# A third edge sum split in two: 1664 destinations by a weighted dense adjacency, the rest by gathering rows

## The chip, the cores and the metric

The kernel runs on one core of a Trainium2 chip. The metric is the device time in microseconds (us) of one execution; lower is better. TensorE, VectorE, ScalarE and GpSimd are called PE, DVE, ACT and POOL in the profile, and SP is the engine that does nothing but start DMAs.

## The reference

The program is two layers of a graph network over 6250 nodes of 256 features and 100,000 edges, sorted by destination, whose destinations are drawn so that low numbers are far more frequent (below node n lie about 100000 * sqrt(n / 6250) edges). Three sums over edges occur: two in the first layer, and this one in the second, with a weight for each edge:

```
feat_norm = sqrt(sum(edge_attr ** 2) + 1e-12);  w = exp(-4 * feat_norm)
agg  = segment_sum(xn[src] * w, dst);  wsum = segment_sum(w, dst)
agg  = agg / max(wsum, 1e-6)
h    = gelu(agg @ W1.T + b1);  y = xn + h @ W2.T + b2;  layernorm(y) * gamma + beta
# beside it, linear attention on the same xn:
k = elu(xn @ Wk.T) + 1;  k_sum = sum over nodes of k;  context = k.T @ v
```

## The kernel before, in words

Nodes are padded to 49 tiles of 128. Stages follow one another, each a block of instruction streams for the engines, joined by semaphores. `second_norm` adds the experts' results to the node rows, normalises them and writes two tables (`x2_tab`, `xn3_tab`); it turns the rows by PE and keeps them turned on the chip (`c.xnT`, 128x2x6272 f32). `gather_third` is the edge sum. `fold_second_attention` and `second_layer_sum` use its result.

All three edge sums go through `aggregate`. An edge tile is 128 edges, and a chunk is four tiles. For each chunk POOL gathers 4x128 rows of the node table, 1 KB each, by indirect DMA (L908) into a ring of `RING` = 5 chunks; DVE makes four one-hot matrices over a window of 128 destinations (L793 with weights in f32, L795 without in fp16); PE multiplies rows by one-hots (L755), eight f32 products a chunk in the third sum; DVE adds the window to the sums on the chip (L763). POOL may start chunk k once chunk k-5 is summed. A chunk's products wait for its rows to land, for its one-hots and for the add of the chunk before the last.

In the third sum all 196 chunks take this way. A `Side` rides in the same loop: `Keys` makes the keys of the linear attention of one node tile per four chunks: ACT copies a tile from `c.xnT` (L2676), PE multiplies (L2647), DVE and ACT make the elu (L2666, L2679, L2671), PE adds products to the attention's sums (L2655, L2658).

The first two sums gather only chunks 98 to 195. The first 1664 destinations (`ND`, 13 tiles) are summed by a dense adjacency that the class `Dense` builds in the same loop: 208 banks of eight destinations, together 710 rows of 128 edges. A row takes two one-hots from DVE (L610, L611) and one fp16 product on PE (L646) into a bank of PSUM; ACT copies the bank to an fp16 adjacency (L631); for every tile of 128 destinations 49 products 128x512 (L663) multiply it by an fp16 node table on the chip (`c.h16`, high and low halves of each feature side by side), 637 in all; DVE adds the two halves, PE turns them, DVE places them (L619, L621, L653, L600). `of_chunk` spreads the banks over the chunks by a cost per bank: early chunks get few banks of many rows, late ones three banks of two rows.

The weight sums per node come from the second gather; `second_norm` inverts them (L2533) and spreads them over the partitions into `c.agg[:, 2]` (L2497), and `second_layer_sum` multiplies on POOL (L2832).

## Time and profile before

| | us |
|---|---|
| Median of 3 runs (lowest, highest) | 4871.57 (4865.47, 4884.47) |
| Profiled execution, its own time | 4901.53 |
| Its span, first to last instruction | 4899.9 |
| Mean granted PE clock, share of full | 0.81 |
| First gather stage, about | 411 to 1124 |
| Second gather stage, about | 1478 to 2093 |
| `second_norm` | 2916 to 3102 |
| Third gather | 3106.2 to 4251.7 |

A time in the trace is counted from the span's start. "Busy" is the time in which at least one instruction of a group runs; "mean" is the length of one, and pipelined instructions overlap, so that count times mean can exceed busy. The idle time of a group is what its engine spent just before its instructions, by what ended it; "issue" is time in which the engine waited for nothing the profile shows, "remote" a release that the profile doesn't name. SPq is SP's queue.

### The profile page before, as it was taken

To read this page: it belongs to the slowest core of one execution; us is meant where nothing else is said; L and a number is where in the kernel's file an instruction comes from. 1 tells how busy PE (TensorE), PEld (TensorE's weight loads), DVE (VectorE), ACT (ScalarE), POOL (GpSimd) and SP (SyncE) were. 2 spreads that over 40 slices of the span, in tenths; PEclk is the share of its full clock that TensorE was granted. 3 is DMA by queue.
4 is the path that set the end of the run, shared out by engine and by line. 5 is a ranking of instruction groups with operands and counts; after the bars stand their busy time and mean duration, and the time that the engine had idled before them with its cause. 6 is when DMAs were issued, how large, how long until landed. Compare 5 with 4: busy or idle time off the path is not lost. (4 is left out here: it accounts for less than half of the span.)

```text
span 4899.9 us, 68142 instructions
## 1 busy us (share of the span) xinstructions
PE 3243.4 (66%) x21190; PEld 2392.1 (49%) x21191; DVE 2407.5 (49%) x7608; ACT 968.5 (20%) x1999; POOL 1955.0 (40%) x2055
## 2 busy tenths in 40 slices
PE   2534888886995768754068861365555656599798
PEld 2422454543564445544057751355555555466554
DVE  7947777663226666566134444322222222277654
ACT  1102222320120112222123322000000000033454
POOL 1013555550005666511711126566666666533100
PEclk8656899997996989976579985677777777789899
DMA  4104232221013323244421117433333333301100
GB/s 122 65 33 144 81 87 84 83 82 48 12 36 99 87 87 87 84 155 160 147 68 64 64 51 227 124 96 97 97 95 97 97 96 95 95 30 45 31 23 26
DMA packets 239100, 416.62 MB, mean 85 GB/s; under 512 B 39042, under 2 KB 171590, under 8 KB 237607
## 3 DMA queue, kind: packets, MB, share of 16 engines
q0 software_dynamic: 90720, 247.45, 17.2%
q1 hardware_dynamic: 141100, 158.88, 9.9%
q10 hardware_dynamic: 7068, 7.60, 0.5%
q8 instruction: 116, 1.90, 0.2%
q14 instruction: 96, 0.79, 0.1%
HBM read 328.87 MB, written 84.91 MB: 84 GB/s over the span
## 5 line engine op out<-in xcount | busy, mean ns | idle before, releaser
L755 PE MATMUL psum<-scr 128*128 128x128 f32 (+1 forms) x5880 | 749.7, 293 | 346.4 <-issue 198.3
L908 POOL DMA_INDIRECT scr<-xn_table,src_i x784 | 746.5, 952 | 410.4 <-issue 239.9
L755 PEld LDWEIGHTS psum<-scr 128*128 128x128 f32 (+2 forms) x5880 | 700.1, 184 | 404.3 <-issue 380.5
L908 POOL DMA_INDIRECT scr<-h_table,src_i x392 | 376.5, 960 | 515.8 <-issue 387.4
L908 POOL DMA_INDIRECT xnT<-xn_table,src_i x392 | 374.1, 954 | 422.2 <-PE psum L755 226.2
L763 DVE TENSOR_TENSOR agg<-agg,psum 128x256 f32 x196 | 82.1, 419 | 728.0 <-remote 538.4
L646 PE MATMUL psum<-scr 128*128 128x98 f16 (+3 forms) x1420 | 262.2, 255 | 262.3 <-DVE scr L611 150.2
L610 DVE TENSOR_SCALAR scr<-iota,scr 128x128 f16<-128x128 bf16 x1420 | 375.0, 272 | 94.7 <-remote 42.7
L611 DVE TENSOR_SCALAR scr<-expert_scores,scr 128x98 f16<-128x98 f16 (+3 forms) x1420 | 397.8, 291 | 1.9 <-issue 1.9
L646 PEld LDWEIGHTS psum<-scr 128*128 128x128 f16 x1420 | 128.5, 100 | 432.0 <-DVE scr L611 229.2
L793 DVE TENSOR_SCALAR scr<-iota,dloc,w_edge 128x128 f32<-128x128 f32 x784 | 221.0, 367 | 83.3 <-issue 77.3
L2435 PE MATMUL psum<-scr,xnT 128*128 128x128 f16 x2544 | 200.4, 234 | 63.1 <-issue 58.6
L2679 ACT ACTIVATE scr<-scr 128x256 f32<-128x256 f32 x49 | 20.4, 416 | 1104.7 <-DVE scr L2666 625.8
L3502 PE MATMUL psum<-scr 128*128 128x512 f16 (+2 forms) x1197 | 209.0, 329 | 16.6 <-ACT scr L3440 9.8
L2435 PEld LDWEIGHTS psum<-scr,xnT 128*128 x2544 | 178.3, 104 | 82.1 <-issue 68.1
L2344 POOL DMA_DIRECT2D expert_results<-scr x106 | 57.3, 541 | 398.6 <-DVE scr L2395 398.6
L1410 PE MATMUL psum<-xnT,scr 128*128 128x512 f32 x392 | 197.7, 650 | 22.0 <-issue 17.7
L631 ACT ACTIVATE agg<-psum 128x392 f16<-128x392 f32 x208 | 103.3, 497 | 524.3 <-PE psum L646 427.9
L631 ACT ACTIVATE scr<-psum 128x392 f16<-128x392 f32 x208 | 100.6, 496 | 497.8 <-PE psum L646 274.1
L663 PE MATMUL psum<-xnT,scr 128*128 128x512 f16 x637 | 181.6, 408 | 3.5 <-DVE agg L600 3.5
L663 PE MATMUL psum<-scr,agg 128*128 128x512 f16 x637 | 173.0, 392 | 0.6 <-DVE agg L600 0.6
L2421 PE MATMUL psum<-ident,scr 128*128 128x128 f32 x212 | 42.3, 284 | 195.2 <-DMA scr<-expert_rows 195.2
(442 smaller groups left out, 5814.6 us busy)
## 6 DMA issues: line engine op xcount, KB each, us to landing
scr<-expert_rows SPq DMA_DIRECT2D x106, 128.0 KB, 2.0
expert_results<-scr POOLq DMA_DIRECT2D x106, 128.0 KB, 2.1
scr<-xn_table,src_i POOLq DMA_INDIRECT x784
agg<-in_L_ffn_W SPq DMA_DIRECT2D x16, 512.0 KB, 9.8
x_table<-scr SPq DMA_DIRECT2D x14, 512.0 KB, 3.0
xn_table<-scr SPq DMA_DIRECT2D x14, 512.0 KB, 4.5
scr<-xn_table SPq DMA_DIRECT2D x14, 512.0 KB, 3.9
scr<-x_table SPq DMA_DIRECT2D x14, 512.0 KB, 4.9
```

Of the source, the lines that this page charges most:

```text
L610: v.tensor_scalar(self.place_hot[:, u, :], c.iota16[:], self.lists[:, 1, r:r + 1], None, ALU.is_equal)
L611: v.tensor_scalar(self.code_hot[:, u, 0:wide], c.iota_wide[:, 0:wide], self.lists[:, 0, r:r + 1], None, ALU.is_equal).then_inc(self.rows_h ...
L631: a.activation(self.adjacency[:, tile % 2, :, q * BN:(q + 1) * BN], self.c.psum[:, 5 + t % 2, 0:BN * HI].rearrange("p (n h) -> p h n", h=H ...
L646: pe.matmul(c.psum[:, 5 + t % 2, at:at + wide * HI], self.place_hot[:, n % self.ring, :], self.code_hot[:, n % self.ring, 0:wide * HI], st ...
L663: last = pe.matmul(c.psum[:, 7, :], self.adjacency[:, tile % 2, h, :], self.x16[:, h, :], start=(h == 0), stop=(h == HI - 1))
L755: last = pe.matmul(bank[b][:, s, :], lhs, hot[:, hot_b, t, :], start=(t == 0 and n == 0), stop=(t == CT - 1 and n == pieces - 1))
L763: return v.tensor_tensor(window, window, bank[b], ALU.add)
L793: last = v.tensor_scalar(hot[:, b, t, :], iota[:], dst(t), weight(t), ALU.is_equal, ALU.mult)
L908: g.indirect_dma_start(out=rows[:, u, t, :], out_offset=None, in_=table, in_offset=bass.IndirectOffsetOnAxis(ap=index(t), axis=0)).then_in ...
L1410: ins = pe.matmul(c.psum[:, 2 + half, :], tile[:, k, :], wkv[:, k, half * 512:(half + 1) * 512], start=(k == 0), stop=(k == 1))
L2435: last = pe.matmul(c.psum[:, 2 + b, m * P:(m + 1) * P], c.w1_16[:, ds(e, 1), k, wp, m * P:(m + 1) * P].rearrange("p e n -> p (e n)"), xT[: ...
L3502: last = pe.matmul(out, weights(wp), moving(xp), start=(first and i == 0), stop=(k_last and i == 2))
```

## The change

`gather_third` gets the form of the first two: chunks 98 to 195 are gathered, and the 1664 first destinations are summed by `WeightedDense`. Since the sum must hold f32 accuracy with weights, each row's place one-hot carries the edge's weight, scaled and already divided by the destination's weight sum, as an fp16 number, and ACT makes a second one with the fp16 rest; PE multiplies both. A bank then holds f32 values: ACT copies them to fp16 (high), and DVE subtracts that from the bank into a second fp16 adjacency (low). For each of 637 slices PE multiplies the high part by 512 columns and the low part by 256. The placed window is written, not added. `second_norm` prepares this: it loads the edge lists, divides the weights, splits them, writes the fp16 node table over `c.xnT`, and sends the turned rows to a table in DRAM (`xnT_tab`), from which `Keys` now loads its tiles (L2676 goes); `Keys` takes two chunks a tile in place of four. `fold_second_attention` loads the weight sums' inverse and the turned rows back. The ring of gathered rows has four chunks.

What moves on PE, in the middle of the third gather. Before, eight L755 are a chunk, L2647 the keys' product, L2655 and L2658 their sums:

```order
L2655 MATMUL psum<-scr 128x256 x2
L2658 MATMUL psum<-ones,scr 128x1 x2
L755 MATMUL psum<-scr 128x128 x8
L2647 MATMUL psum<-scr 128x256 x2
L755 MATMUL psum<-scr 128x128 x24
L2655 MATMUL psum<-scr 128x256 x2
```

Now, late in the stage, where L870 is the chunk, L759 and L762 are a row's two products (high and low weight), L773 and L775 a slice by the high and by the low adjacency:

```order
L759 MATMUL psum<-scr 128x392
L762 MATMUL psum<-scr 128x392
L773 MATMUL psum<-xnT,agg 128x512
L775 MATMUL psum<-xnT,scr 128x256
L773 MATMUL psum<-xnT,agg 128x512
L775 MATMUL psum<-xnT,scr 128x256
L773 MATMUL psum<-xnT,agg 128x512
L775 MATMUL psum<-xnT,scr 128x256
L870 MATMUL psum<-scr 128x128 x8
L2862 MATMUL psum<-scr 128x256 x2
L2865 MATMUL psum<-ones,scr 128x1 x2
L759 MATMUL psum<-scr 128x392
```

Between two chunks PE now has one to five such turns, and a step of the keys after every chunk.

On SP's queue, from the third gather's end to the constants of the last stage, before:

```order
L2708 DMA scr<-turned_weights 128x512 x2
L2703 UNCONDITIONAL_BRANCH
L2803 UNCONDITIONAL_BRANCH
L2806 DMA scr<-turned_weights 128x512 x3
L2809 DMA scr<-in_L_gnn_b 128x256
```

and now:

```order
L2923 DMA scr<-turned_weights 128x512 x2
L2925 DMA agg<-wsum_row 128x896
L2927 DMA xnT<-xnT_table 128x2x896
L2925 DMA agg<-wsum_row 128x5376
L2927 DMA xnT<-xnT_table 128x2x5376
L2918 UNCONDITIONAL_BRANCH
```

Four loads, 9.6 MB together, stand on the queue ahead of the last stage's constants.

The diff, cut to its core:

```diff
+HOTR3, RING3 = 8, 4
+WSCALE = 2.0 ** 15
...
+            gathered = c.base[:, FIRST // CT:NC]
+            step.done(v.tensor_scalar(gathered, gathered, float(ND), None, ALU.max))
...
+class WeightedDense(Dense):
...
+    def vector(self, v, t):
+        c = self.c
+        tile = self.places(t)
+        if tile is not None:
+            v.wait_ge(self.turned, tile + 1)
+            v.tensor_scalar(c.agg[:, 0:2, tile * P:(tile + 1) * P], c.psum[:, 7, 0:2 * P].rearrange("p (k n) -> p k n", n=P),
+                            1.0 / (XS * WSCALE), None, ALU.mult).then_inc(self.placed, 1)
+        if 0 <= t - 2 < NB:
+            v.wait_ge(self.taken, t - 1)
+            v.tensor_tensor(self.nodes(self.low, t - 2), self.bank(t - 2), self.nodes(self.adjacency, t - 2), ALU.subtract
+                            ).then_inc(self.lowered, 1)
+        if t < NB:
+            for r in BANK_ROWS[t]:
+                n = self.row_at[r]
+                u = n % self.ring
+                if n >= self.ring:
+                    v.wait_ge(self.rows_used, n - self.ring + 1)
+                wide = HI * ROW_OF[r][1]
+                v.tensor_scalar(self.place_hot[:, u, 0, :], c.iota16[:], self.list_at("low", r), self.list_at("weight", r),
+                                ALU.is_equal, ALU.mult)
+                v.tensor_scalar(self.code_hot[:, u, 0:wide], c.iota_wide[:, 0:wide], self.list_at("code", r), None,
+                                ALU.is_equal).then_inc(self.rows_hot, 1)
+        self.add_halves(v, t)
...
+    def scalar(self, a, t):
+        if 0 <= t - 1 < NB:
+            tile, q = divmod(t - 1, BPT)
+            a.wait_ge(self.rows_used, self.row_at[BANK_ROWS[t - 1][-1]] + 1)
+            if tile >= 2 and q == 0:
+                a.wait_ge(self.sliced, (tile - 1) * self.SLICES)
+            a.activation(self.nodes(self.adjacency, t - 1), self.bank(t - 1), ACT.Copy).then_inc(self.taken, 1)
+        if t < NB:
+            for r in BANK_ROWS[t]:
+                n = self.row_at[r]
+                u = n % self.ring
+                a.wait_ge(self.rows_hot, n + 1)
+                a.activation(self.place_hot[:, u, 1, :], self.place_hot[:, u, 0, :], ACT.Copy, scale=self.list_at("ratio", r)
+                             ).then_inc(self.rows_low, 1)
+    def tensor(self, pe, t):
+        c = self.c
+        if t < NB:
+            for r in BANK_ROWS[t]:
+                n = self.row_at[r]
+                node, wide, k, count = ROW_OF[r]
+                at = (node % BN) * HI
+                u = n % self.ring
+                pe.wait_ge(self.rows_hot, n + 1)
+                if r == BANK_ROWS[t][0] and t >= 2:
+                    pe.wait_ge(self.lowered, t - 1)
+                out = c.psum[:, 5 + t % 2, at:at + wide * HI]
+                pe.matmul(out, self.place_hot[:, u, 0, :], self.code_hot[:, u, 0:wide * HI], start=(k == 0), stop=False,
+                          skip_group_check=True)
+                pe.wait_ge(self.rows_low, n + 1)
+                pe.matmul(out, self.place_hot[:, u, 1, :], self.code_hot[:, u, 0:wide * HI], start=False,
+                          stop=(k == count - 1), skip_group_check=True).then_inc(self.rows_used, 1)
+        self.turn_sums(pe, t)
...
             for h in range(HI * q // self.SLICES, HI * (q + 1) // self.SLICES):
-                last = pe.matmul(c.psum[:, 7, :], self.adjacency[:, tile % 2, h, :], self.x16[:, h, :], start=(h == 0),
-                                 stop=(h == HI - 1))
+                pe.matmul(c.psum[:, 7, :], self.adjacency[:, tile % 2, h, :], self.x16[:, h, :], start=(h == 0), stop=False,
+                          skip_group_check=True)
+                last = pe.matmul(c.psum[:, 7, 0:D], self.low[:, tile % 2, h, :], self.x16[:, h, 0:D], start=False,
+                                 stop=(h == HI - 1), skip_group_check=True)
...
-                    if dense and dense.placed_by[min(k + 2, n_chunks)]:
-                        v.wait_ge(dense.placed, dense.placed_by[min(k + 2, n_chunks)])
...
-                        g.wait_ge(summed, fast.summed(k - RING + 1))
+                    if k >= ring:
+                        g.wait_ge(summed, fast.summed(k - ring + 1))
...
-            sp.dma_start(c.agg[:, 2, :], c.wsum_row.partition_broadcast(P)).then_inc(w_out, 16)
+            sp.dma_start(inverse, c.wsum_dense.partition_broadcast(P)).then_inc(inverse_in, 16)
+            sp.wait_ge(w_vec, 4)
+            sp.dma_start(wsum_rows[0:DT, :], dense_scale[0:DT, :]).then_inc(w_out, 16)
+            sp.dma_start(wsum_rows[DT:NT, :], wsum[DT:NT, :]).then_inc(w_out, 16)
...
-            v.memset(c.agg[:, 0:2, :], 0.0)
...
+            v.memset(c.agg[:, 0:2, ND:NP], 0.0)
+            step = Chain(v, listed)
+            v.wait_ge(lists_in, 16)
+            step.done(v.tensor_tensor(by_place, c.iota[:, 0:BN].unsqueeze(1).broadcast_to([P, ROWS, BN]),
+                                      place.unsqueeze(2).broadcast_to([P, ROWS, BN]), ALU.is_equal))
+            step.wait()
...
+                last = v.tensor_tensor(of_bank, of_bank, nodes.unsqueeze(2).broadcast_to([P, e - b, m, BN]), ALU.mult)
...
+            step.done(v.tensor_reduce(of_row, by_place, AX.X, ALU.add))
+            step.wait()
+            step.done(v.scalar_tensor_tensor(w_valid, w_valid, WSCALE, of_row, ALU.mult, ALU.mult))
+            step.wait()
+            step.done(v.tensor_copy(high16, w_valid))
+            step.wait()
+            step.done(v.tensor_copy(high, high16))
+            step.wait()
+            step.done(v.tensor_tensor(rest, w_valid, high, ALU.subtract))
+            step.done(v.tensor_scalar(of_row, high, 1e-30, None, ALU.max))
+            step.wait()
+            step.done(v.reciprocal(of_row, of_row))
+            step.wait()
+            for slot, j, values in ((0, 0, code), (0, 1, low), (1, 0, high)):
+                v.tensor_copy(c.list_parts[slot][:, :, j], values)
+            v.tensor_tensor(c.list_parts[1][:, :, 1], rest, of_row, ALU.mult)
...
+            def low_part(s, h):
+                nt = HALVES[h][1]
+                v.wait_ge(high_ready, s * 2 + h + 1)
+                tiles16 = rows16[:, ds(s * TS + HALVES[h][0], nt), :]
+                v.scalar_tensor_tensor(tiles16[:, :, D:2 * D], xn3[:, h, 0:nt, :], XS, tiles16[:, :, 0:D],
+                                       ALU.mult, ALU.subtract).then_inc(low_ready, 1)
...
+                if former is not None:
+                    low_part(*former)
...
+            def spill(s, h):
+                t0, nt = HALVES[h]
+                a.wait_ge(copied, s * 2 + h + 1)
+                a.dma_start(turned_tab[:, :, ds(s * SS + t0 * P, nt * P)], xn3T[:, h, :, 0:nt * P]).then_inc(spilled[h], 16)
+            def unit(s, h, former, last):
+                t0, nt = HALVES[h]
+                if not last:
+                    a.wait_ge(vec, s * (2 * PER) + h * PER + 2)
+                    indices(s + 1, h)
+                if former is not None:
+                    spill(*former)
+                a.wait_ge(vec, s * (2 * PER) + h * PER + 5)
+                a.activation(rstd[:, h, 0:nt], rstd[:, h, 0:nt], ACT.Sqrt).then_inc(root, 1)
+                a.wait_ge(vec, s * (2 * PER) + (h + 1) * PER)
+                a.activation(rows16[:, ds(s * TS + t0, nt), 0:D], xn3[:, h, 0:nt, :], ACT.Copy, scale=XS).then_inc(high_ready, 1)
+                a.wait_ge(turned, s * 2 + h + 1)
+                a.wait_ge(spilled[h], s * 16)
+                for k in range(2):
+                    ins = a.activation(xn3T[:, h, k, 0:nt * P], c.psum[:, 2 * h + k, 0:nt * P], ACT.Copy)
+                ins.then_inc(copied, 1)
...
+    hot, rows_f = part.take([HOTS, CT, W]), part.take([RING3, CT, D])
+    wk, tile, rows = c.m0, part.take([2, P]), part.take([D])
     low, e, kk = part.take([D]), part.take([D]), part.take([D])
-    beyond = part.take([ET - FIRST])
+    place_hot, code_hot = part.take([HOTR3, 2, P], F16), part.take([HOTR3, BN * HI], F16)
+    adjacency_low = part.take([2, HI, P], F16)
+    adjacency = c.agg[:, 2, :].bitcast(F16).rearrange("p (a h n) -> p a h n", a=2, h=HI)
...
-            v.tensor_scalar(beyond, c.dloc[:, FIRST:ET], 0.0, MASKED, ALU.is_lt, ALU.mult).then_inc(unmasked, 1)
-            v.wait_ge(unmasked, 1)
-            v.tensor_tensor(c.dloc[:, FIRST:ET], c.dloc[:, FIRST:ET], beyond, ALU.add)
...
-        turn, steps = 4, 0
+        turn, steps = 2, 2
...
-            if u == 0:
-                a.wait_ge(z_ready, i)
-                a.activation(tile[:], c.xnT[:, :, ds(i * P, P)], ACT.Copy).then_inc(tile_ready, 1)
-            if u == 1:
+            if u == 1 and new:
...
+            sp.dma_start(tile, turned_tab[:, :, 0:P]).then_inc(tile_ready, 16)
+            sp.dma_start(rows, c.xn3_tab[0:P, :]).then_inc(rows_ready, 16)
+            with sp.Fori(1, NT) as i:
+                sp.wait_ge(z_ready, i)
+                sp.dma_start(tile, turned_tab[:, :, ds(i * P, P)]).then_inc(tile_ready, 16)
                 sp.wait_ge(sums_done, i)
                 sp.dma_start(rows, c.xn3_tab[ds(i * P, P), :]).then_inc(rows_ready, 16)
-    aggregate(c, c.xn3_tab, hot, rows_f, split=False, weighted=True, slots=(0, 1), side=Keys())
+    dense = WeightedDense(c, "conv3", c.h16, adjacency, adjacency_low, c.list_parts, place_hot, code_hot,
+                          NC - FIRST // CT, HOTR3)
+    aggregate(c, c.xn3_tab, hot, rows_f, split=False, weighted=True, slots=(0, 1), side=Keys(), dense=dense,
+              start=FIRST // CT, unset=c.agg[:, 0:2, 0:ND])
...
+            for n, nodes in enumerate((slice(0, SS), slice(SS, NP))):
+                sp.dma_start(c.agg[:, 2, nodes], c.wsum_row[:, nodes].partition_broadcast(P)
+                             ).then_inc(c.last_wsum_loaded[n], 16)
+                sp.dma_start(c.xnT[:, :, nodes], c.xnT_tab.rearrange("p (k n) -> p k n", k=2)[:, :, nodes]
+                             ).then_inc(c.last_xnT_loaded[n], 16)
...
+                g.wait_ge(c.last_wsum_loaded[0 if isinstance(s, int) and s == 0 else 1], 16)
...
+                pe.wait_ge(c.last_xnT_loaded[0 if isinstance(s, int) and s == 0 else 1], 16)
```

## Rows read from the trace of the kernel before

**Rows 1.** Stretches: length, busy PE, PEld, DVE, ACT, POOL, PE clock, DMA share, GB/s.

```profile
411.00:1124.00 713.00, 589.62 (x3668) 343.58 (x3667) 479.45 (x2180) 176.24 (x352) 374.07 (x392) 0.91 0.29 83
...
1478.00:2093.00 615.00, 446.61 (x4117) 309.49 (x4117) 380.38 (x1949) 100.60 (x208) 376.47 (x392) 0.87 0.30 86
...
2915.90:3102.20 186.30, 24.54 (x98) 18.97 (x98) 85.63 (x206) 34.09 (x68) 110.27 (x99) 0.50 0.60 191
...
3106.20:4251.70 1145.50, 682.40 (x3728) 619.58 (x3726) 315.47 (x1078) 36.53 (x99) 746.49 (x784) 0.75 0.33 96
```

**Rows 2.** Groups by line, third gather; busy us, mean ns, idle before.

```profile
L908 POOL DMA_INDIRECT scr<-xn_table,src_i x784 | 746.5, 952 | 410.4 <-issue 239.9 <-remote 139.7 <-PE psum L755 30.9
...
L793 DVE TENSOR_SCALAR scr<-iota,dloc,w_edge 128x128 f32<-128x128 f32 x784 | 221.0, 367 | 83.3 <-issue 77.3 <-PE psum L755 3.0 <-PEq L2616 3.0
```

**Rows 3.** Timeline of the third gather near its end: start, length, engine, line.

```profile
4242.84 1.03 PE L2647 MATMUL psum<-scr 128*128 128x256 f32 x4
...
4246.61 0.42 DVE L2666 TENSOR_SCALAR scr<-psum 128x256 f32<-128x256 f32 x1
...
4246.84 3.81 PE L755 MATMUL psum<-scr 128*128 128x128 f32 x32 [1.20 <-DVE agg L763]
...
4250.49 1.03 PE L2655 MATMUL psum<-scr 106*128 106x256 f32 x4
...
4251.35 0.50 PE L2658 MATMUL psum<-ones,scr 106*128 106x1 f32 x4
```

**Rows 4.** Timeline of the second gather, which has the dense part.

```profile
1800.90 0.34 PE L646 MATMUL psum<-scr 128*128 128x98 f16 x4
...
1801.08 1.03 PE L663 MATMUL psum<-xnT,scr 128*128 128x512 f16 x4
...
1807.20 1.87 PE L663 MATMUL psum<-xnT,scr 128*128 128x512 f16 x4
...
1704.62 0.24 DVE L610 TENSOR_SCALAR scr<-iota,scr 128x128 f16<-128x128 bf16 x1
...
1704.78 0.24 DVE L611 TENSOR_SCALAR scr<-expert_scores,scr 128x98 f16<-128x98 f16 x1
```

**Rows 5.** Groups of the second gather by line and form.

```profile
L631 ACT ACTIVATE scr<-psum 128x392 f16<-128x392 f32 x208 | 100.6, 496 | 497.8 <-PE psum L646 274.1 <-remote 183.1 <-issue 35.9
...
L762 DVE SCALAR_TENSOR_TENSOR agg<-psum,agg 128x384 f32 x98 | 54.0, 551 | 70.9 <-remote 46.4 <-PE psum L755 24.0 <-DVE agg L600 0.5
```

**Rows 6.** Waits in the first gather: who waited for whom, us, times, longest.

```profile
DVE xnT L1426 <- ACT xnT L1447: 126.1, 37, 5.4
```

**Rows 7.** Timeline in the experts' stage: four ScalarE operations.

```profile
2906.20 1.14 ACT L2361 ACTIVATE scr<-psum,feature_columns 128x128 f32<-128x128 f32 x4 [3.70 <-PE psum L2435]
```

**Rows 8.** Timeline of the start of the normalisation.

```profile
2929.50 11.68 POOL L2523 DMA_INDIRECT scr<-expert_results,scr  x1 [0.30 <-issue]
...
2929.75 10.51 DVE L2529 MEMSET agg<- 128x12544 f32 x1 [14.60 <-issue]
...
2943.02 0.35 SPq L2497 DMA_DIRECT2D agg<-wsum_row  x1
...
2959.49 1.23 DVE L2539 TENSOR_TENSOR scr<-scr 128x1024 f32<-128x1024 f32 x1 [18.17 <-DMA scr<-x_table]
```

**Rows 9.** Lengths: DVE over all 5680 list elements; a reciprocal.

```profile
L1214 DVE TENSOR_TENSOR agg<-agg x1: 6077/6077/6077, 331.7 to 331.7; 128x5680 f32<-128x5680 f32 x1
...
L2908 DVE RECIPROCAL scr<-scr x14: 303/328/353, 4284.6 to 4567.3; 128x32 f32<-128x32 f32 x7, 128x24 f32<-128x24 f32 x7
```

**Rows 10.** Timeline: a 3136 KB load and its wait; the last stage's constants.

```profile
2092.62 0.32 SPq L1773 DMA_DIRECT2D scr<-dis_row  x1
...
2104.75 13.29 DVE L1781 TENSOR_TENSOR agg<-agg,scr 128x6272 f32<-128x6272 f32 x2 [12.41 <-DMA wsum_row<-agg]
...
4252.13 0.81 SPq L2708 DMA_DIRECT2D scr<-turned_weights  x2
...
4270.11 6.15 PE L3087 MATMUL psum<-xnT,scr 128*128 128x512 f32 x8 [9.91 <-DMA scr<-in_L_ffn_gW]
```

288 lines of the change are left out of this document (175 added, 113 removed).

## The prediction, made before the changed kernel ran

> **What bounds the kernel now.** I read the busy times by stretch first, then, for the third gather, its groups by line and its timeline, and beside it the same views of the first two gathers, which already have a dense part. The table of stretches [rows 1] shows the third gather as much the longest stage, 1145.5 us, with PE 60% busy at a mean granted clock of 0.75, DVE 28% and POOL 65%. POOL's group [rows 2] says what the stage runs on: 784 gathers of 0.952 us with about 0.3 us between two, so 1.25 us each at best, and waits on top for chunks summed ("remote" and PE L755). 1145.5 / 784 = 1.46 us for a gather; the DMA moves 96 GB/s meanwhile. So the stage is bound by gathers and their landing, and PE and DVE wait for them. The second gather [rows 1] has 392 gathers with the dense part beside them in 615 us, 1.57 us each, hardly more; the first one has 392 in 713 us, 1.82 each, and there PE (590 busy) and DVE (479) are fuller. The change turns the third stage into the form of these two, with more arithmetic than either.
>
> **The change part by part.** The profiled execution took 4901.53 us against a median of 4871.57 for the runs shown. The sum is made on the profiled execution, and the difference is taken from the median.
>
> *Gathers.* 392 instead of 784. By the present rate 392 x 1.46 = 572 us, by POOL's own pace 392 x 1.25 = 490. These are floors of the new stage; the question is whether PE or DVE is now above them. The ring of four chunks instead of five leaves POOL three chunks ahead; at over 7 us a chunk (below) that is over 21 us for four gathers of 5 us in all, so I price it at nothing; if PE were fast again, its cost would be the gathers' rate.
>
> *PE at full clock.* A chunk's eight f32 products: two chunks in 3.81 us [rows 3], 1.9 each, x 98 = 187 us. Slices: four of 512 columns take 1.03 us at the full clock and 1.87 at half [rows 4], so what scales with the clock is 0.84 / 4 = 0.21 us each; 637 x 0.21 = 134, and 637 of 256 columns half of it, 67. Row products: four of 98 columns begin within 0.18 us (1800.90 to 1801.08, [rows 4]), 0.045 each. The 710 rows are 16 of 49 columns, 323 of 98, 285 of 196 and 86 of 392, each now twice, together 244,000 columns: 112 us. Keys: 1.03 + 1.03 + 0.50 [rows 3] x 49 = 125. Turning the tiles, about 6. Sum 631 us. That is above both floors: PE becomes the bound.
>
> *DVE.* Row one-hots start 0.16 us apart [rows 4]. The place one-hot now has two scalar operands and a multiplication, a form the trace has only in f32, 0.367 us [rows 2]. Its bounds are 0.16 and 0.37; I take 0.2. 710 x (0.2 + 0.16) = 256. The 208 subtractions from a PSUM bank of 392 columns: nearest is L762, 0.55 us at 384 columns [rows 5], 114. Chunk one-hots 392 x 0.28 (221.0 / 784 [rows 2]) = 110. Window adds, keys' two steps, tile sums and placing: 98 + 98 + 39 of 0.42 [rows 3] = 99. Sum 579, bounds 551 to 700. So DVE lies beside PE, 50 us below it, but not evenly: `of_chunk` gives the first 18 chunks 6 to 34 rows with few slices, where DVE is longer, and the late ones three turns, where PE is (8 us against 5.5). Taking the larger of the two chunk by chunk costs about 25 us over PE's sum.
>
> *ACT.* Low one-hots 710 x 0.285 (1.14 / 4 [rows 7]) = 202, banks 208 x 0.496 [rows 5] = 103, exponentials 49 x 0.42 = 20: 325, far from a bound. But it stands in the chain: it copies bank t-1 only after PE has finished it, and makes the low one-hots of turn t after that, some 0.5 + 0.1 + 0.3 us, and 0.285 a row. PE has 3.5 slices x 0.315 = 1.1 us to cover the first; a second or third turn in one chunk with four rows loses some 0.4 us. I take 33 us for all. The very first bank has 34 rows, each going DVE, ACT, PE before the first chunk can be summed: 34 x 0.45 = 15 us at the start.
>
> *Clock.* It was 0.91 and 0.87 in the first two gathers and 0.75 in this one [rows 1]. PE will be fuller than in the first, so 0.93: 631 / 0.93 = 678. The stage: 678 + 25 + 33 + 15 = 751, with a few us to drain 755 us. Saved: 1145.5 - 755 = 390. Bounds of the stage: 680 (PE alone) to 878 (rival one).
>
> *The normalisation.* At the start DVE clears two thirds of `agg` in 10.5 us, and POOL's gather beside it takes 11.68 instead of 0.95 [rows 8]. The new clearing is 9216 of 12544 columns, 7.7 us. Behind it, in one chain on DVE before the first unit: three passes over 5680 elements at 6.1 [rows 9], the middle one in eight pieces (+1), 19; a reciprocal of 710 elements at (353 - 303) / 8 = 6.2 ns each [rows 9], 4.5; ten operations on 710 elements at 0.5 to 0.9, 7; small ones and waits, 2. From 2929.75 that ends at 2970; the first unit began at 2959.49, when its rows landed [rows 8]: +10. Their load will land earlier, as the 3.2 MB spread no longer stands ahead of it, so nothing else is late. In the seven passes each adds 2 DVE operations for the low rows of the table (1.23 at 1024 columns [rows 8], 0.9 at 768) and 0.9 MB of turned rows sent out on ACT's queue into a stage that moves 191 GB/s: 4.8 us of traffic, of which I take 2 as not hidden. 7 x 4 = 28, and 2 for the last spill. The fp16 copies on ACT lie in its wait for PE's turning. Sum +40; bounds +12 (start alone) to +75 (all of the traffic too, and ACT in the chain).
>
> *The fold.* SP works its loads in order: the first rows of the normalisation, asked for just behind the 3.2 MB spread of 2943.02, landed after 16 us [rows 8]. A 3136 KB load took 12.1 us from issue to its waiter [rows 10], about 3.8 us a MB. The change puts 9.6 MB on the queue at 4253; at 3.1 to 3.8 us a MB they are in at 4283 to 4289, and the last stage's constants come behind, 4 us. PE now begins that stage at 4270.11 [rows 10], waiting for just these constants. +21; bounds 0 (the later loads overtake) to +30.
>
> *The rest.* Two DVE operations at the start of the third gather go, -1. The ACT copy of the keys' tile and the gathers' window waits lay beside other work: 0. In the first two gathers waits between DVE's own operations go: 0 to -3.
>
> Sum: -390 + 40 + 21 - 1 = -330. 4871.57 - 330 = **4541 us**.
>
> A rule of the Trainium skill speaks against this change. First the row: POOL's gathers take 0.954 and 0.960 us in the first two stages, beside 1420 and more one-hots of 16-bit numbers each, and 0.952 in the third, with none of that form (busy over count [rows 1]). So small one-hots don't hold POOL here, though the long clearing did [rows 8]. SBUF — State Buffer, "Who interferes with whom", says that VectorE in a two-port perf mode and GpSimd lock each other out of a shared port pair for a whole instruction; taken for every one-hot it would give rival three.
>
> **The rivals.**
>
> *One: the engines don't overlap as well as summed.* The first gather by the same prices: an f32 product costs about four times an fp16 one of as many columns, so the four key and value products of 512 columns are 4 x 4 x 0.21 = 3.4 us a tile, 167 for 49; four f32 products of 128 for each tile, some 1.1 us, 54; slices 134; rows 56; 98 chunks of 16 fp16 products of 128, 16 x 0.053, 83; 6 for turning: 500 us of PE. The stage took 713, 1.4 times as much. At that ratio 631 gives 883, 128 us more: 4669. Against it: there DVE sat idle 126 us for ACT's squares of the same step [rows 6], which held up its dense turns; the new keys leave a chunk between PE's product, DVE and ACT. For it: the new turn waits on DVE, ACT and PE in a ring, and the first stage's clock of 0.91 is in that ratio too.
>
> *Two: gathers still bound.* If row and slice products hide in the weight loads' shadow, the stage falls to 392 x 1.46 = 572 to 1.57 x 392 = 615 as in the second gather: saving 530 to 573, 4871.57 - 550 + 60 = 4382. Against: PE's sum is a count of columns.
>
> *Three: DVE and POOL exclude one another.* 392 x 0.95 = 372 us of POOL beside 579 of DVE, one after the other: 951, 4737. Against: the stages above.
>
> *Four, slower than before: PE stays at the lower clock level, 1.2 GHz, through the stage.* In the third gather now the mean is 0.75, so it is at each of its two levels half of the time; a chunk in the middle of the stage is as often slow as fast. With small waits inside every turn it may not come up. 631 x 2 + 73 = 1335 us, 190 more than now, plus 60: 5121. It decides from a mean clock of 631 / (1145 - 60 - 73) = 0.62 downwards. Against: in both stages with the dense part the clock is higher, not lower [rows 1].
>
> *Five: the change doesn't take effect*, as when the flag sends the sums down their slow way; then the time would be many times this. The dense part covers all edges of its destinations by the counts, and chunk 98 begins near node 1574, below 1664: 0.01.
>
> **How the numbers follow.** Forecast 0.68 (its own range 4470 to 4625), rival one 0.16, two 0.07, three 0.04, four 0.03, five 0.01, and 0.01 for a gain in the stage eaten by an unseen cost elsewhere to within nothing. The range that leaves out two in ten reaches over rival one's size but not over two or three: 4440 to 4685. Half a percent, 24 us, is about what a measurement tells from no change here. Faster by more: 0.95; within: 0.01; slower: 0.04.
>
> **What would show it.** The new third gather at 755 us with PE busy over 85% and a clock over 0.9; POOL waiting for PE in nearly every chunk, not for landings. Late chunks longer (about 8.5 us) than middle ones (about 7); were they alike at 6, gathers bind. DVE's idle before its bank subtractions and the row products' idle "<-ACT" give the ring's price (33 us). The one-hot with two scalars: near 0.2 us apart. The first unit of the normalisation 10 us later, a pass of it 4 us longer. PE's first product of the last stage some 20 us behind the fold's end. Wrong would be a stage under 680 (PE's prices too high) or a clock under 0.8.

## The result and the profile after

The changed kernel takes 4527.3 us, the median of four runs (4524.13 to 4538.25), against 4868.52 for the kernel before on the same chip (four runs, 4863.0 to 4884.47): a ratio of 0.9297, 95% interval 0.9274 to 0.9321, so 341 us less. 4541 was predicted, 330 less. The profiled execution took 4538.25 us, with a span of 4536.6.

The stretches of the changed kernel, in the columns of [rows 1]: length, busy time of PE, PEld, DVE, ACT and POOL, granted clock, DMA share, GB/s.

```profile
411.00:1475.00 1064.00, 881.98 (x4688) 528.63 (x4687) 587.24 (x2361) 230.69 (x426) 380.48 (x395) 0.91 0.23 68
1475.00:2091.10 616.10, 444.90 (x4117) 305.87 (x4117) 380.43 (x1949) 100.45 (x208) 375.55 (x391) 0.87 0.31 90
2903.30:3109.80 206.50, 24.54 (x98) 18.98 (x98) 127.16 (x242) 33.28 (x71) 114.10 (x100) 0.51 0.62 199
3114.20:3869.50 755.30, 681.97 (x4877) 510.80 (x4876) 574.40 (x2255) 353.20 (x968) 374.05 (x392) 0.93 0.30 86
3870.00:3904.00 34.00, 4.46 (x15) 3.21 (x14) 2.38 (x8) 0.00 (x0) 2.37 (x2) 0.50 0.93 361
3904.00:4536.00 632.00, 562.37 (x2716) 357.47 (x2716) 381.91 (x712) 275.50 (x435) 110.62 (x70) 0.90 0.10 32
```

The third gather is the fourth line: 755.3 us where it was 1145.5 [rows 1], PE busy 90% at a clock of 0.93, DVE 76%, POOL down from 746 to 374. The fold, the fifth line, is new as a stretch with DMA busy 0.93 of the time.

The waits of that stage, by who waited for whom (us, times, longest):

```profile
POOL scr L1020 <- PE psum L870: 256.9, 85, 11.6
DVE scr L714 <- ACT agg L737: 66.9, 50, 3.1
PEld psum L762 <- ACT scr L743: 52.3, 157, 6.8
PE psum L762 <- ACT scr L743: 19.7, 30, 6.7
PE psum L759 <- DVE scr L726: 17.8, 12, 2.8
```

POOL waits 85 times, in 98 chunks, for PE to have summed a chunk. PE is now what the others wait for. The groups of the stage that carry the prediction's prices (busy, mean ns of one, idle before):

```profile
L743 ACT ACTIVATE scr<-scr,agg 128x128 f16<-128x128 f16 x710 | 247.3, 394 | 63.7 <-DVE scr L726 41.3 <-issue 17.4
L724 DVE TENSOR_SCALAR scr<-iota,agg 128x128 f16<-128x128 bf16 x710 | 228.5, 325 | 33.8 <-remote 17.2 <-issue 9.2 <-PE psum L762 7.4
L762 PE MATMUL psum<-scr 128*128 128x98 f16 (+3 forms) x710 | 156.6, 247 | 31.1 <-ACT scr L743 19.7 <-issue 3.3
L714 DVE TENSOR_TENSOR scr<-psum,agg 128x392 f16<-128x392 f32 x208 | 116.9, 562 | 67.8 <-ACT agg L737 66.9 <-issue 0.7
```

**Where the time went.** Between fixed marks of the two profiled executions: up to the experts' last send (POOL, 2915.90, now 2903.30) -12.6; from there to the third gather's first one-hot 190.3, now 210.9 (+20.6); the third gather to the fold's first copy 1146.0, now 756.4 (-389.6); the fold to PE's first product of the last stage 17.9, now 33.3 (+15.4); the rest +2.9. Together -363.3. The two medians are 341 apart: the profiled execution of before was 30 us above its median, that of after 11. So about 20 us of the sum of the marks belongs to the two executions, and the first term, -12.6, is not larger than that.

### The profile page after: what moved, and what is told of

Read it like the earlier page. It is cut to its first block and busy times, and to the rows that moved or that the text cites. A ratio compares the mean times of both kernels' runs of the same rounds, so it can differ in the third digit from the quotient of the medians.

```text
span 4536.6 us, 72069 instructions
## 1 busy us (share of the span) xinstructions
PE 3246.4 (72%) x22342; PEld 2281.7 (50%) x22343; DVE 2707.3 (60%) x8818; ACT 1283.5 (28%) x2871; POOL 1587.1 (35%) x1664
## 3 DMA queue, kind: packets, MB, share of 16 engines
q0 software_dynamic: 71904, 196.05, 14.6%
## 5 line engine op out<-in xcount | busy, mean ns | idle before, releaser
L1020 POOL DMA_INDIRECT scr<-xn_table,src_i x392 | 374.0, 954 | 382.3 <-PE psum L870 256.9
L870 PE MATMUL psum<-scr 128*128 128x128 f16 (+1 forms) x4312 | 409.3, 258 | 7.4 <-remote 5.0
L870 PEld LDWEIGHTS psum<-scr 128*128 128x128 f16 (+2 forms) x4312 | 390.4, 145 | 39.0 <-issue 11.4
L743 ACT ACTIVATE scr<-scr,agg 128x128 f16<-128x128 f16 x710 | 247.3, 394 | 63.7 <-DVE scr L726 41.3
L724 DVE TENSOR_SCALAR scr<-iota,agg 128x128 f16<-128x128 bf16 x710 | 228.5, 325 | 33.8 <-remote 17.2
L773 PE MATMUL psum<-xnT,agg 128*128 128x512 f16 x637 | 222.3, 387 | 0.6 <-DVE agg L710 0.6
L726 DVE TENSOR_SCALAR scr<-expert_scores,agg 128x98 f16<-128x98 f16 (+3 forms) x710 | 197.6, 280 | 0.0
L2507 DVE SCALAR_TENSOR_TENSOR scr<-psum,scr 128x256 f32<-128x256 f32 x106 | 45.0, 425 | 240.1 <-PE psum L2560 240.1
```

Source lines behind the costliest of these rows:

```text
L724: v.tensor_scalar(self.place_hot[:, u, 0, :], c.iota16[:], self.list_at("low", r), self.list_at("weight", r), ALU.is_equal, ALU.mult)
L743: a.activation(self.place_hot[:, u, 1, :], self.place_hot[:, u, 0, :], ACT.Copy, scale=self.list_at("ratio", r)).then_inc(self.rows_low, 1)
L773: pe.matmul(c.psum[:, 7, :], self.adjacency[:, tile % 2, h, :], self.x16[:, h, :], start=(h == 0), stop=False, skip_group_check=True)
L870: last = pe.matmul(bank[b][:, s, :], lhs, hot[:, hot_b, t, :], start=(t == 0 and n == 0), stop=(t == CT - 1 and n == pieces - 1))
L1020: g.indirect_dma_start(out=rows[:, u, t, :], out_offset=None, in_=table, in_offset=bass.IndirectOffsetOnAxis(ap=index(t), axis=0)).then_in ...
```

## The experiments

They ran on three chips, which are of two kinds by the kernel before. "The second chip" stands for two of them: experiments 1 to 4 ran on one, where the kernel before takes 4617 us, and 9 to 12 on the other, where it takes 4612. Experiments 5 to 8 ran on a chip where it takes 4872; which chip gave the result above is not recorded, but the 4869 us there are alike, and both are called "the first chip". Each ratio is to the kernel before on the same chip, and stage lengths are compared within one of the two kinds.

**1. No low one-hots** (second chip). In the third gather ACT makes no low one-hot and PE reads the high one again (the low half of the weights is left out; the scale is halved).

```
-                pe.wait_ge(self.rows_low, n + 1)
-                pe.matmul(out, self.place_hot[:, u, 1, :], ...
+                pe.matmul(out, self.place_hot[:, u, 0, :], ...
-                a.activation(self.place_hot[:, u, 1, :], self.place_hot[:, u, 0, :], ...
```

> ACT makes no low one-hots; the second row product of TensorE reads the high one-hot again, so PE has all its products and the ring DVE - ACT - PE of a row is cut by ACT (the low half of the weights is left out). Changed kernel: 4527 us, third gather 755 us. Theory A (prediction: the ring costs 33 us beside PE's sum): 4494, stage about 722. Theory B (PE is nearly the whole bound, 682 of 755 us busy, and its idle time is the start and the end of the stage): at most 12 us less, 4515 to 4527. Theory C (ACT's copies of banks come late because they stand behind the one-hots): over 45 us less.

4336.8 us, ratio 0.9395 (0.9379 to 0.9410); the stage took 685.3 us against 714.3 in experiment 3, which has this stage as the changed kernel. 29 us: theory A. The edit takes away ACT's work and PE's wait for it together; experiments 7, 9 and 10 ask which of them counts.

**2. No low slices** (second chip). The 256-column products of the adjacency's low half are left out, and that part of the sum with them.

```
-                pe.matmul(c.psum[:, 7, :], self.adjacency[...], self.x16[:, h, :], start=(h == 0), stop=False, ...
-                last = pe.matmul(c.psum[:, 7, 0:D], self.low[...], self.x16[:, h, 0:D], start=False, ...
+                last = pe.matmul(c.psum[:, 7, :], self.adjacency[...], self.x16[:, h, :], start=(h == 0), stop=(h == HI - 1), ...
```

> The 637 products of 256 columns with the low half of the adjacency are left out (so is that part of the sum). Theory A (prediction: PE is the bound, each costs its columns, 0.105 us at full clock): 67 / 0.95 = 70 us less, 4457, and the stage near 685 with PE still over 85% busy. Theory B (these products hide behind the weight loads of 0.10 us): their whole price is the load, same order, 60 to 70 us, but not told apart by this. Theory C (the ring of DVE, ACT and PE binds, PE's share is only full by chance): under 30 us less, and PE's busy share falls to under 85%.

4319.8 us, ratio 0.9358 (0.9343 to 0.9374); the stage took 674.0, 40 less, between A and C. The stretches tell why (experiment 2, then 3; columns as above):

```profile
3150.00:3300.00 150.00, 141.29 (x1056) 103.67 (x1055) 140.12 (x583) 91.46 (x251) 88.24 (x94) 0.95 0.36 102
3450.00:3600.00 150.00, 138.78 (x902) 94.79 (x902) 120.92 (x445) 74.72 (x196) 77.47 (x82) 0.97 0.31 91
```

```profile
3150.00:3300.00 150.00, 143.38 (x1155) 109.70 (x1153) 135.34 (x563) 88.25 (x245) 86.13 (x92) 0.97 0.35 100
3450.00:3600.00 150.00, 141.30 (x998) 106.59 (x997) 110.53 (x409) 69.19 (x182) 71.47 (x75) 0.95 0.29 82
```

In the first half DVE is busy 135 of 150 us beside PE, and with the slices gone 140. Counted by the chunks' window additions, 34 of 42 us come from the last 52 chunks and 7 from the first 45: in the chunks before them DVE is about as near to being the bound as PE.

**3. The large loads later** (second chip). Nothing is left out.

```
             for n, nodes in ((0, slice(0, SS)), (1, slice(SS, NP))):   # fold_second_attention: now n = 0 only
...
             for h in range(2):
                 load(0, h, True)
+            load_last(c, sp, 1, slice(SS, NP))    # second_layer_sum: wsum_row and xnT_table
```

> The two large loads of the fold (8.2 of 9.6 MB, nodes after the first 1024 or so) are issued on the same queue behind the last stage's constants and first rows; nothing is left out. Changed kernel: PE's first product of the last stage comes 33.4 us after the fold's first DVE copy, before 18. Theory A (the constants stand in one queue behind the 9.6 MB): 12 to 17 us less, 4510 to 4515, that stretch back at 18 to 21 us. Theory B (the time goes to the DMA engines' total traffic in this place, whatever the order): no change, since the same bytes are moved in the same time, 4525. Theory C (the second pass of the last stage then waits for its rows behind 8 MB): what is gained at the start is lost by 3990.

4349.8 us, ratio 0.9424 (0.9409 to 0.9440). SP's issues in the changed kernel, and PE's first product of the last stage (start, length):

```profile
3870.62 0.69 DVE L2932 COPY scr<-psum 128x512 f32<-128x512 f32 x1 [4.69 <-PEq L898]
3873.17 0.58 SPq L2927 DMA_DIRECT2D xnT<-xnT_table  x1
3882.46 4.21 SPq L3029 DMA_DIRECT2D scr<-in_L_mix_bproj  x1
3886.71 6.32 SPq L3029 DMA_DIRECT2D scr<-in_L_ffn_gb  x1
3893.07 3.21 SPq L3030 DMA_DIRECT2D scr<-in_L_ffn_gW  x1
3903.95 6.46 PE L3309 MATMUL psum<-xnT,scr 128*128 128x512 f32 x8 [25.21 <-DMA scr<-in_L_ffn_gW]
```

And with the loads later:

```profile
3715.40 0.43 SPq L3031 DMA_DIRECT2D scr<-in_L_mix_bproj  x1
3715.88 0.43 SPq L3031 DMA_DIRECT2D scr<-in_L_ffn_gb  x1
3716.35 0.43 SPq L3032 DMA_DIRECT2D scr<-in_L_ffn_gW  x1
3722.36 2.93 PE L3312 MATMUL psum<-xnT,scr 128*128 128x512 f32 x3 [10.68 <-DMA scr<-in_L_ffn_gW]
```

Behind the large loads even the issuing of a small one takes 3 to 6 us instead of 0.43. The fold, from its first copy (3703.64 here) to that product, falls to 18.7 us, from 33.3 in the changed kernel and 33.2 in experiment 4 on this chip: theory A. It stays gained: experiment 4, which lacks this edit, is 17.4 us longer.

**4. Gathers held back at the start** (second chip).

```
                 for k in range(n_chunks):
+                    if k == 1 and dense and not dense.loads:
+                        g.wait_ge(dense.rows_used, len(BANK_ROWS[0]))
```

> In the third gather POOL issues the first chunk's four gathers and then waits until the 34 rows of the first bank have been multiplied, before it goes on; nothing is left out. In the changed kernel the first 22 rows take 7 us, then seven come 1.0 to 3.0 us apart with DVE idle and nobody late, until POOL has filled its ring (last gather at 3133.05), and the first chunk is summed 27 us after the stage begins, where 15 were predicted. Theory A (DVE's instructions come in by DMA and are held up by the gathers' transfers): the 34 rows take about 14 us, the stage begins 8 to 13 us earlier, 4515 to 4519. Theory B (the instructions are late whatever POOL does): no gain, or 5 us lost since chunks 1 to 3 land later, 4527 to 4532.

4367.3 us, ratio 0.9458 (0.9443 to 0.9474). The edit could not be judged: on this chip the first bank's rows took 12.9 us with it and 13.0 without it (experiment 3). On the first chip they took 26.4 to 26.9 in all five profiles of kernels with this stage. DVE's one-hots there, in the changed kernel:

```profile
3122.75 0.32 DVE L724 TENSOR_SCALAR scr<-iota,agg 128x128 f16<-128x128 bf16 x1 [0.96 <-PE psum L762]
3127.68 0.31 DVE L724 TENSOR_SCALAR scr<-iota,agg 128x128 f16<-128x128 bf16 x1 [2.33 <-remote]
3131.18 0.33 DVE L724 TENSOR_SCALAR scr<-iota,agg 128x128 f16<-128x128 bf16 x1 [3.02 <-remote]
3137.20 0.31 DVE L724 TENSOR_SCALAR scr<-iota,agg 128x128 f16<-128x128 bf16 x1
3140.60 3.16 DVE L908 TENSOR_SCALAR scr<-iota,dloc,w_edge 128x128 f32<-128x128 f32 x12
```

From 3121 to 3137 a row comes every 0.6 to 3.5 us, with PE and ACT waiting for DVE; from 3137 on it is 0.38 again, 4 us after POOL's last gather (3133.05) into the filled ring. That DVE's instructions reach it late beside the gathers would fit, but was not shown.

**5. The changed kernel again** (first chip).

> The changed kernel once more, as the reference of the runs beside it, on the chip where they run. On the chip of the last four runs the kernel before took 4617 us where it took 4869 before, and the second gather 496 us where it took 587 to 596. Theory A (there a gather lands as fast as POOL issues it, 1.27 us, so that the kernel before gains most in its third gather of 784): changed kernel 4362 to 4370 and a ratio of 0.945, the gain 250 us instead of 341. Theory B (all stages are faster alike): ratio 0.93.

4531.2 us, ratio 0.9295 (0.9279 to 0.9311), third gather 751.1 us. It is the reference for 6 to 8, and the expectation's figure for the second chip was not tested by it; there experiment 4, whose edit moved nothing, stands nearest, at 0.9458.

**6. The waits put back** (first chip) into the first two gathers.

```
             v.wait_ge(self.turned, tile + 1)
+            v.wait_ge(added, settled)
...
+                    if dense and dense.loads and dense.placed_by[min(k + 2, n_chunks)]:
+                        v.wait_ge(dense.placed, dense.placed_by[min(k + 2, n_chunks)])
                     add_window(v, ...)
```

> The changed kernel with the waits put back that the first two gathers had between DVE's own operations (on the last window added, and on the tile placed); nothing is left out. In the first pair of profiles the changed kernel reached the end of the experts 12.6 us earlier, 4 us of it in the first gather and 8 to 9 in the second; predicted were 0 to 3. Theory A (these waits are the cause): 8 to 13 us more than the changed kernel, a ratio to before higher by 0.002 to 0.003. Theory B (the difference is that of two executions or of code positions, and the waits cost 0 to 3 us): same time within 3 us.

4527.5 us, ratio 0.9297 (0.9280 to 0.9313), not told from experiment 5: theory B. The clearing begins at 2918.5, as in the changed kernel (2920.2 and 2919.0).

**7. Low products two rows behind** (first chip), with the edit of experiment 3. A region of the bank is now begun before the one ahead of it has had its low product, and the sums come out changed; the work is the same, and the time is what is read.

```
+                behind.append(r)
+                if len(behind) > 2:
+                    low_product(behind.pop(0))
+            for r in behind:
+                low_product(r)
```

> Two edits: the fold's two large loads behind the last stage's constants (alone: PE's first product 18.7 us after the fold's start, not 33.4), and PE multiplies a row's low one-hot two rows later than its high one, so that it does not wait for ACT inside a bank; nothing is left out. Without ACT's one-hots the third gather took 685 us against 714. Theory A (the 29 us are PE waiting for ACT row by row): the stage falls by 15 to 25 us to 690 to 700 on that chip, the whole 28 to 40 below the changed kernel. Theory B (the 29 us come at the end of a bank: last low product, ACT's copy, DVE's subtraction, then the slices): 5 us or less from this edit, and 13 to 20 for both.

4509.3 us, ratio 0.9255 (0.9242 to 0.9267), 22 below experiment 5. By the marks, the fold gave 14.8 of it (33.6 to 18.8) and the last stage 7.4; the third gather took 752.8 against 751.1. So nothing from this edit: theory B. PEld's wait for ACT ahead of the low product fell from 46.9 to 21.1 us, and its wait for DVE ahead of the high product rose from 17.6 to 37.5: the wait only moved.

**8. Twice the turned rows** (first chip) sent out in the normalisation.

```
                 a.dma_start(turned_tab[...], xn3T[:, h, :, 0:nt * P]).then_inc(spilled[h], 16)
+                a.dma_start(again_tab[...], xn3T[:, h, :, 0:nt * P]).then_inc(spilled[h], 16)
```

> In the normalisation each turned tile is sent out twice, the second time to a table of its own, on the same queue (0.9 MB more a pass, 6.4 MB in all). Predicted was 4 us a pass for the added work, 2 of them for this traffic; measured were about 1.4 a pass in all, counted from the experts' end to the third gather 20 us, 10 of them at the start. Theory A (the traffic costs its bytes at the stage's 191 GB/s, 4.8 us a pass, of which half shows): 14 us more, 28 with ACT's queue waiting for it. Theory B (loads and sends have room, the pass is set by its chain): 0 to 4 us more.

4534.0 us, ratio 0.9307 (0.9291 to 0.9322), not told from experiment 5. By the marks, the first unit to the third gather's first one-hot takes 167.9 us against 156.5: 11.4, or 1.6 a pass. In the whole they don't show: in this profiled execution the third gather is 2 us shorter and the last stage 6. Between A and B.

**9 and 10. One wait a row; one wait for two rows** (second chip, both with the edit of experiment 3). PE waits for ACT's low one-hot alone, ahead of both products, for one row or for two.

```
-                pe.wait_ge(self.rows_hot, n + 1)
+                if (r - BANK_ROWS[t][0]) % 2 == 0:      # 1 in experiment 9
+                    pe.wait_ge(self.rows_low, min(n + 2, self.row_at[BANK_ROWS[t][-1]] + 1))
...
-                pe.wait_ge(self.rows_low, n + 1)
```

> The fold's loads reordered as before (14.6 us by its stretch), and PE waits once a row in place of twice: only for ACT's low one-hot, which is itself made after the high one, ahead of both products (710 waits fewer); nothing is left out. On the chip of the reference run the changed kernel takes 4531 us and its third gather 751 to 756 (749 to 753 in its variants); without ACT's one-hots, and with one wait a row, the stage was 29 us shorter, 0.4 us a chunk also in the late chunks of six rows. Theory A (the second wait between two short products costs PE about 0.04 us, since it breaks the run of weight loads and products): the stage falls by 20 to 30 us, the whole 35 to 45 below the changed kernel. Theory B (ACT's own time counts: the bank's copy stands behind its one-hots, and frees the bank late): stage unchanged or up to 20 us longer, as the high product now waits for ACT too; the whole 0 to 15 below.

> As the one with one wait a row, but PE waits for two rows at once (355 waits), then issues four products; nothing is left out. Theory A (each wait costs PE about 0.04 us): 10 to 14 us less than with one wait a row, 45 to 60 below the changed kernel. Theory B (the chain through DVE and ACT counts, and PE now starts a bank one row later, about 0.4 us for each of 208 banks where it is not hidden): the same as with one wait a row or up to 40 us more.

One wait a row: 4350.0 us, 0.9426 (0.9413 to 0.9439), the same as experiment 3. 710 waits fewer gave none of the 20 to 30 us of theory A, which falls. That a wait costs nothing is not quite shown, since the high product now waits for ACT too: PE's idle time ahead of the row products is 37.7 us, against 32.3 in experiment 3. For pairs: 4374.3 us, 0.9483 (0.9470 to 0.9496), 24 more. The same idle time is 69.4 us: ahead of a bank's first product 45.4 in place of 27.2, and ahead of its later pairs 24.0 in place of 10.5. So the later one-hots cost, and the larger part of it at a bank's start. The stage in experiments 9 and 10:

```profile
2991.30:3705.20 713.90, 666.71 (x4880) 497.16 (x4878) 571.52 (x2255) 361.25 (x968) 373.11 (x392) 0.96 0.32 91
```

```profile
2989.90:3729.00 739.10, 662.11 (x4880) 504.28 (x4878) 573.30 (x2255) 358.56 (x968) 373.29 (x392) 0.94 0.31 88
```

Equal work, 25 us apart. Counted by the chunks' window additions, 17.7 of 24.6 fall into the last 52, where 20 of experiment 1's 29 fell too.

**11. Clearing later** (second chip), with the edits of experiment 10.

```
-            v.memset(c.agg[:, 0:2, ND:NP], 0.0)
             step = Chain(v, listed)
...
             unit(0, 1, (0, 0))
+            v.memset(c.agg[:, 0:2, ND:NP], 0.0)
```

> As with pairs, and the clearing of agg (7.74 us) is moved from ahead of the lists to behind the second unit of the normalisation; nothing is left out. Theory A (the start's one chain on DVE sets the first unit, and a pass of 21 us has room for 7.7 us of DVE, which is 127 of 206 us busy): 7 to 8 us less. Theory B (it moves into a pass that DVE's chain sets, and a gather of POOL beside it takes 12 us instead of 1): 0 to 2 us less or some us more.

4367.4 us, 0.9466 (0.9453 to 0.9479), 6.9 less than experiment 10, whose highest and lowest runs (4369.7 to 4380.6) overlap these (4363.1 to 4370.4) by 0.7. From DVE's first instruction to the first unit it is 33.5 us against 40.3, and to the third gather 6.3 less: theory A, though by the runs alone the two would hardly be told apart.

**12. The kernel before again** (second chip), one run.

> The kernel before once more, for its profile. The changed kernel twice reached its 7.7 us clearing at 2919 to 2920, the kernel before its 10.5 us clearing at 2929.75, and the waits put back did not bring these 10 us back. Theory A (they are the difference of one execution): the clearing of this run begins between 2917 and 2923. Theory B (they belong to the kernel before, by the windows of the first two gathers that it adds below node 1664, or by where its code lies): again 2927 to 2932, the second gather 596 us against 587.

4612.8 us. The clearing begins at 2797.9, and in the changed kernel's variants of that chip at 2800 to 2805 behind 3 us of new small work: no 10 us here, so theory A as far as this chip goes; the kernel before was not profiled again on the first chip, where the 10 us were. Its third gather, and POOL's waits in it; then those on the first chip, with PE's wait for DVE, which has no counterpart on the second:

```profile
2971.30:3964.60 993.30, 655.58 (x3728) 601.88 (x3726) 318.81 (x1077) 36.15 (x98) 746.21 (x784) 0.80 0.38 111
```

```profile
POOL scr L908 <- issue: 248.6, 758, 18.0
POOL scr L908 <- PE psum L755: 7.9, 26, 0.3
```

```profile
POOL scr L908 <- issue: 239.9, 720, 19.2
POOL scr L908 <- remote: 139.7, 51, 4.4
POOL scr L908 <- PE psum L755: 30.9, 13, 3.4
PE psum L755 <- DVE agg L763: 134.4, 35, 15.4
```

On the second chip POOL hardly waits for PE: 784 gathers in 993 us, 1.27 each, its own pace. There the changed stage (714 us) saves 279, not 390, and the whole some 250.

What held the stage on the first chip was not the landing of the rows. The last DMA packet of a gather ends 1.48 us (median) after POOL's instruction on the first chip and 1.47 on the second. But PE's first product of a chunk follows the chunk's landing by 11.3 us (median) on the first and by 0.43 on the second. POOL waits for a summed chunk, and there PE is late. One chunk's products on the first chip, whose rows had landed at 3691.4, and one on the second, whose rows landed at 3485.2:

```profile
3704.95 0.19 PEld L755 LDWEIGHTS psum<-scr 128*128 128x128 f32 x1 [0.94 <-issue]
3705.66 0.27 PE L755 MATMUL psum<-scr 128*128 128x128 f32 x1 [1.16 <-issue]
3706.37 0.36 PE L755 MATMUL psum<-scr 128*128 128x128 f32 x1 [0.44 <-issue]
3709.18 0.37 PE L755 MATMUL psum<-scr 128*128 128x128 f32 x1 [1.83 <-issue]
```

```profile
3485.79 3.65 PE L755 MATMUL psum<-scr 128*128 128x128 f32 x16 [2.36 <-issue]
```

Inside a chunk nothing makes PE wait, and yet it stops. Counted over the stage, PE is idle 133 times for over 0.3 us, 125.8 us in all, ahead of products that wait for nothing; in the third gather of experiment 12 and in that of the changed kernel, on either chip, never. The stage is 152 us longer than on the second chip. Why PE stops on the first chip, and why in the changed kernel it doesn't, stays open.

## Why the prediction was right, step by step

**Gathers as a floor.** Right for the new stage: 392 x 1.25 = 490 is below it, and POOL waits for PE. The reading of the old stage was wrong: 1.46 us a gather was put down to gathers and their landing, with PE and DVE waiting for them. On this chip POOL waited for PE, which stopped without a cause that the profile shows (12). The pace of POOL alone gives 993 us, as on the second chip. The forecast took the 1145.5 us as measured, so the wrong reading did it no harm here.

**PE's sum.** 631 us at full clock and 0.93 gave 678; PE is busy 682 at 0.93. Leaving out the low slices gives back 40 us and not their 70, since DVE is close behind.

**DVE's sum.** 579; measured 574. The one-hot with two scalars stands 0.22 ahead of its fellow, 0.2 taken; the subtraction takes 0.562, 0.55 taken. ACT's low one-hots run 0.29 apart; ACT is busy 353, of 325.

**Unevenness, ring, start.** +25 + 33 + 15 were added to 678. The ring's price is 29 us (experiment 1). Its place was given as single rows and turns; fewer waits of PE (9) and another order inside a bank (7) gave nothing, and later one-hots cost 24 us (10), more at a bank's start than behind it. Which link of DVE, ACT and PE is last was not separated. The start was mis-sized: 26.4 us where 15 was taken; on the second chip 13.0. That the stage came out at 756.4 of 755 is luck in part. Beside PE's busy time 73 us are left, just the 73 that were added. But on the second chip, in experiment 4, the stage takes 711.8 with PE busy 668.0, and 44 are left: 29 for the ring and 13 for the start leave 2 for the unevenness, an estimate, where 25 were taken. The first chip's stage is 44 us longer than that: 13 at the start, 29 in the next 45 chunks and 2 in the rest, and no term stood for that. By the window additions, chunks 60 to 90 take 8.0 us, 30 to 60 take 7.2, and the first thirty 7.3 on the first chip and 6.5 to 6.6 on the second; predicted were 8.5 for late and 7 for middle ones.

**Clock.** Right at 0.93; rival four, at half clock, was far off.

**Normalisation.** +40 predicted, +20.6 by the marks, the step's size being wrong. The start was right: the first unit comes 53.5 us behind the experts' last send, before 43.6, so +9.9 for 10. Two small errors cancel in it: the clearing begins 3 us later by small work ahead of it that had no term, and from there to the first unit it takes 36.6 us where 40 were added up. Its chain on DVE in the changed kernel:

```profile
2920.16 7.74 DVE L2675 MEMSET agg<- 128x9216 f32 x1 [1.87 <-issue]
2927.82 6.00 DVE L2679 TENSOR_TENSOR scr<-iota,agg 128x5680 f32<-128x5680 f32 x1
2933.86 6.56 DVE L2691 TENSOR_TENSOR scr<-scr,agg 128x272 f32<-128x272 f32 x8
2940.45 6.07 DVE L2695 TENSOR_REDUCE agg<-scr 128x710 f32<-128x5680 f32 x1
2950.01 4.59 DVE L2706 RECIPROCAL agg<-agg 128x710 f32<-128x710 f32 x1
2956.76 1.22 DVE L2724 TENSOR_TENSOR scr<-scr 128x1024 f32<-128x1024 f32 x1
```

The passes were not: 157.4 us from the first unit to the third gather against 146.7, 1.5 us a pass in place of 4. Doubling the traffic costs 1.6 a pass (8), so the 2 us for the traffic look about right, and the DVE operations priced beside it, 2 a pass, hidden; no run left those out.

**Fold.** +21 predicted, +15.4 measured, 14.6 given back by the order of the loads (3). The mechanism stood as written; 3.1 to 3.8 us a MB was too dear, since at the 361 GB/s that the stretch moved a MB takes 2.8. PE's product comes 24.5 us behind the fold's last copy, where 20 were named as the sign.

**The first two gathers.** 0 to -3; the marks show -12.6, but the waits put back cost nothing (6), and it does not come back on the second chip (12). Where the 12.6 come from on the first is open.

**The rivals.** One would need 1.4 times PE's sum; it is 1.20. Two fell: the slice products have their price (2), and POOL waits for PE. Three fell too: POOL's gathers take 0.954 us beside 2255 DVE instructions (374.0 / 392).

**The sum.** Against the marks' -363 the predicted -330 is short by 33: 19 in the normalisation, 6 in the fold, 11 ahead of the experts' end, less 3 in the last stage. Against the medians' -341 it is short by 11, since 22 belong to the two profiled executions. The third gather's -390 has no part in it.

**A version faster than both.** Experiment 3 alone: 0.9424 on the second chip, where the changed kernel's nearest stand-in has 0.9458. Its loads with the later clearing of 11 would be some 7 us better by the two runs; the pair was not run.

## What to carry to other kernels

Price the engine that will bind after the change by counting its columns and rows, and check the bound you remove as well: a rate of 1.46 us a gather looked like landings, and the time from landing to first use (11.3 us, against 0.43 on another chip) says that it was not. What there was to save differed by 110 us between two chips. Large loads for later belong behind the small ones needed next, in the same queue. In a ring over three engines take away work and add latency in separate runs: the busy shares do not show which of the two is paid for.

## What the hardware showed that was not expected

The prediction took it from [rows 8] that the clearing holds up POOL. In the changed kernel a gather that starts 1.8 us into it takes 12.69 us, though the one before it, also inside it, takes 0.95; and it ends 0.8 us behind the list comparison that follows. With the clearing moved (experiment 11), the same 7.74 us have five gathers of 0.94 to 0.95 inside them, and a long gather of 6.00 us stands beside the comparison:

```profile
2921.95 12.69 POOL L2660 DMA_INDIRECT scr<-expert_results,scr  x1 [0.30 <-issue]
```

```profile
2801.59 6.08 DVE L2677 TENSOR_TENSOR scr<-iota,agg 128x5680 f32<-128x5680 f32 x1 [2.86 <-DMA agg<-edge_lists]
2802.49 6.00 POOL L2660 DMA_INDIRECT scr<-expert_results,scr  x1 [0.30 <-issue]
2845.01 7.74 DVE L2750 MEMSET agg<- 128x9216 f32 x1 [1.87 <-issue]
2846.77 0.95 POOL L2660 DMA_INDIRECT scr<-expert_results,scr  x1 [0.31 <-issue]
```

So this clearing by itself holds up nothing, and the comparison, which reads two operands from SBUF, does. The Trainium skill, SBUF — State Buffer, "Who interferes with whom", says just that: a VectorE instruction with two SBUF inputs contends with a GpSimd instruction that reads SBUF. The 6.00 us agree; that the gather of 12.69 us was held from 6 us before the comparison began does not follow from it. DVE's next instruction, the comparison, waits for the edge lists, and in all eleven traces that record their landing the gather that is held is the first one begun after it. In the changed kernel the lists landed at 2921.05, and the gathers began at 2920.70 (0.95 us long) and 2921.95; in experiment 3 the landing was at 2801.08 and the gathers began at 2801.01 and 2802.27. So an instruction that stands ready behind the clearing may hold POOL before it runs. That could also be behind the gather of 11.68 us beside the old clearing ([rows 8], and again in experiment 12), which has small DVE operations right behind it; the old clearing's form, 12544 elements in one run and not two rows of 4608, is the rival. No run separates them.

Two Trainium2 chips differ by 5% on the kernel before (spans 4899.9 and 4611.1), 270 of the 289 us in its three gathers: from first gather to last the second takes 596 us on one and 494 on the other. In the third it is PE and DVE that are late, not the rows (experiment 12).
